# A block of attention and adapters: the row maxima turned by VectorE instead of TensorE and ScalarE, with other places for the side work

## The reference

```python
mod = (silu(c) @ wmod).reshape(4, 6, 1, 256)          # sa, ca, ga, sb, cb, gb
h = layernorm(x) * (1 + ca) + sa
x = x + ga * attention(h)                             # 16 heads of 16 features
h = layernorm(x) * (1 + cb) + sb
x = x + gb * ffn(h)

def attention(h):
    q, k, v = heads(h @ qkv_w.T)
    p = softmax(q @ k.T * 0.25)                       # over 1024 keys
    return merge(p @ v) @ proj_w.T + proj_b

def ffn(x):                                           # x: [batch, 1024, 256] as 16 x 256 x 256 or 4 x 1024 x 256
    h = relu(x @ W_enc + b_enc)                       # 8 experts of 64
    losses = mean((h @ W_dec + b_dec - x) ** 2)       # per batch and expert
    e = argmin(losses)                                # one expert for a batch
    return x @ W_base + b_base + relu(x @ W_down[e] + b_down[e]) @ W_up[e] + b_up[e]
```

## Time and profile before

| | |
|---|---|
| median of three runs | 971.41 us (971.34 to 973.51) |
| the profiled execution | 969.45 us |
| its span | 967.6 us |
| TensorE matmuls, weight loads busy | 933.6 us (96%), 487.8 us (50%) |
| VectorE, ScalarE, GpSimd busy | 791.9 us (82%), 656.6 us (68%), 373.1 us (39%) |
| mean granted clock of TensorE | 0.987 |

### The profile page before, as it was taken

One profiled execution on the slowest core, in us unless ns is written; L12 is line 12 of the kernel. 1 busy time (PEld: TensorE's weight loads), 2 busy tenths in 40 slices (PEclk: granted clock), 3 DMA queues, 4 the chain that ended last, 5 costly groups with the idle time before them and its releaser, 6 DMA issues.

```text
span 967.6 us, 16714 instructions
## 1 busy us (share of the span) xinstructions
PE 933.6 (96%) x5890; PEld 487.8 (50%) x5890; DVE 791.9 (82%) x1629; ACT 656.6 (68%) x1295; POOL 373.1 (39%) x497
## 2 busy tenths in 40 slices
PE   6899999999999999999999999999999999999998
PEld 5443444444445555555454555555445455644486
DVE  4799989999888888877897987876887778888365
ACT  2148788888688677666779677675777766657930
POOL 4050265226456454121756545121655321115320
PEclk9889999999999999999999999999999999999999
DMA  6933052253454211555150511536133500141001
GB/s 179 144 73 45 23 111 63 57 116 87 77 83 74 58 42 36 73 92 162 46 94 13 94 57 36 83 65 167 46 67 51 78 12 25 46 128 55 30 6 50
DMA packets 51427, 68.78 MB, mean 71 GB/s; under 512 B 12347, under 2 KB 35648, under 8 KB 51332
## 3 DMA queue, kind: packets, MB, share of 16 engines
q1 hardware_dynamic: 50108, 66.84, 32.1%
q0 software_dynamic: 384, 0.79, 0.6%
q10 hardware_dynamic: 852, 0.09, 0.1%
HBM read 29.31 MB, written 12.59 MB: 43 GB/s over the span
## 4 chain that ended last, share of the span: by engine, by line
PE 75%; DVE 11%; ACT 5%; DMA 4%; SPq 3%; issue 2%; POOL 1%; ACTq 0%; DVEq 0%
PE pE L851 25%; PE pM L851 21%; PE pO L851 20%; DVE mx L1350 7%; PE pX L851 7%; DMA QO<-lo 2%; ACT P L1176 2%; SPq L1955 1%; DMA xin<-in_x 1%; DVE junk L1544 1%; ACT h2l_full L1263 1%; SPq L2015 1%; DMA P<-in_wmod 0%; ACT h1l_full L1217 0%; DVE junk L1487 0%
## 5 line engine op out<-in xcount | busy, mean ns | idle before, releaser
L1350 DVE TENSOR_REDUCE mx<-pM 128x1 f32<-128x512 f32 x458 | 298.9, 683 | 41.6 <-PE pM L851 39.4
L1176 ACT ACTIVATE P<-pM 128x512 f32<-128x512 f32 x464 | 260.2, 603 | 71.5 <-PE pM L851 70.1
L1350 DVE TENSOR_REDUCE mx<-pE 128x1 f32<-128x512 f32 x428 | 284.5, 682 | 29.4 <-PE pE L851 28.4
L1176 ACT ACTIVATE P<-pE 128x512 f32<-128x512 f32 x413 | 240.6, 603 | 81.0 <-PE pE L851 79.9
L851 PE MATMUL pO<-P,V 128*17 128x512 f32 x2048 | 260.6, 604 | 0.3 <-ACT P L1176 0.2
L851 PE MATMUL pM<-KO,QO 48*128 48x512 f32 x458 | 181.7, 451 | 7.7 <-DMA QO<-lo 6.0
L851 PE MATMUL pE<-KO,QO 48*128 48x512 f32 x428 | 178.4, 444 | 1.4 <-DVE mx L1350 0.6
L851 PE MATMUL pM<-QO,KO 50*128 50x512 f32 x464 | 173.6, 433 | 0.9 <-DVE mx L1350 0.4
L851 PE MATMUL pE<-QO,KO 50*128 50x512 f32 x413 | 169.8, 438 | 1.3 <-DVE mx L1350 0.7
L851 PEld LDWEIGHTS pM<-QO,KO 50*128 50x128 f32 x464 | 80.2, 187 | 85.3 <-issue 59.6
L851 PEld LDWEIGHTS pE<-QO,KO 50*128 50x128 f32 x413 | 73.5, 186 | 96.9 <-issue 76.4
(11 more groups left out here) (362 smaller groups left out, 1392.5 us busy)
## 6 DMA issues: line engine op xcount, KB each, us to landing
outs<-osb SPq DMA_DIRECT2D x31, 256.0 KB, 2.0
KO<-hi SPq DMA_DIRECT2D x56, 128.0 KB, 4.0
QO<-hi SPq DMA_DIRECT2D x56, 128.0 KB, 5.6
x<-in_x SPq DMA_DIRECT2D x20, 256.0 KB, 3.5
out<-x SPq DMA_DIRECT2D x16, 256.0 KB, 2.1
AT<-outs SPq DMA_DIRECT2D x15, 256.0 KB
asum<-wsum SPq DMA_DIRECT2D x15, 256.0 KB
KO<-lo SPq DMA_DIRECT2D x28, 128.0 KB, 4.0
```

Of the source, the lines that this page charges most:

```text
L1176: e.activation(P[:, u % 3, j, :], bank(s), ACT.Exp).then_inc(*empties(s))
L1350: e.tensor_reduce(mx[:, hq % 2, k:k + 1, kh], bank(s), AX.X, ALU.max, negate=True).then_inc(*empties(s))
```

## The change

The step `mturn` is done by VectorE. It reads `mhl` and writes `mT` by four transposes of 32 by 32 elements; there is no matmul, no bank and no copy. A new semaphore `s_mT` counts the turns and takes the place of the bank's semaphores for SyncE, for ScalarE's first two DMAs and for VectorE's own reductions. `mturn` is now a quiet step, put in front of the quiet queue, two units behind `mmax`. Beside that, constants of the order are changed.

```diff
-SHORT = {"ln1turn", "mturn", "oturn", "atturn", "xturn", "select", "modT2"}
+SHORT = {"ln1turn", "oturn", "atturn", "xturn", "select", "modT2"}
-SHARE = (1.3, 1.8, 2.2, 2.4)
+SHARE = (1.3, 1.8, 1.6, 2.4)
-LIGHT = 66
+LIGHT = 68
...
     for gi in range(3, 4 * NB):
-        u = 200 if gi == 4 * NB - 1 else 16 * gi - 33
+        u = 196 if gi == 4 * NB - 1 else 16 * gi - 35
         at(u, ("qk", gi // 4, gi % 4, 0), ("qk", gi // 4, gi % 4, 1))
         if gi > 3:
-            at(u - 9, ("wqload", gi), ("wqs", gi))
+            at(u - 12, ("wqload", gi), ("wqs", gi))
...
-            at(B + 5, ("pick", q), ("select", q), ("fetch", q))
+            at(B + 7, ("pick", q), ("select", q), ("fetch", q))
...
-            u = B + (20 if b == LAST else 53)
+            u = B + (20 if b == LAST else 49)
             at(u, ("prep", b), ("wbload", b))
...
-                at(B + 16, ("ln1load", b + 1, k), ("ln1s", b + 1, k), ("ln1n", b + 1, k), ("ln1turn", b + 1, k), ("h1s", b + 1, k))
-            at(B + 34 if b else B + 18, *(("v", b + 1, k) for k in range(4)))
+                at(B + 10, ("ln1load", b + 1, k), ("ln1s", b + 1, k), ("ln1n", b + 1, k), ("ln1turn", b + 1, k), ("h1s", b + 1, k))
+            at(B + 37 if b else B + 18, *(("v", b + 1, k) for k in range(4)))
...
     if kind == "mturn":
-        return [(("mmax", b), 1.2)]
+        return [(("mmax", b), 2)]
...
     if kind == "qk":
-        return ... + [(("moved", 4 * b + a[0] - 1), 4 if (b, a[0]) == (1, 2) else 3)]
+        return ... + [(("moved", 4 * b + a[0] - 1), 4 if (b, a[0]) == (1, 2) else 2)]
...
     if kind == "ehi":
-        return [(("enc", b, a[0]), 0.5)] + ...
+        return [(("enc", b, a[0]), 0.4)] + ...
...
-                waiting["short"].insert(0, ("mturn", m // 32 - 1))
+                waiting["quiet"].insert(0, ("mturn", m // 32 - 1))
...
-        for _ in range(6 if moving and moving[0][1] == 4 * NB - 1 else 3):
+        for _ in range(6 if moving and moving[0][1] == 4 * NB - 1 else 2):
...
-                elif kind == "mturn":                      # TensorE
-                    pe.wait_ge(s_mhl, s[1] + 1)
-                    e.transpose(o[0:32, 0:128], mhl[:, s[1] % 2, :], ident).then_inc(*fills(s))
...
-                elif kind == "mturn":                      # ScalarE
-                    hq = s[1]
-                    if hq >= 2:
-                        for j in range(4):
-                            act.wait_ge(d_m[hq % 2][j], 16 * (hq // 2))
-                    act.wait_ge(*full(*s))
-                    e.activation(mT[0:32, hq % 2, :], bank(s)[0:32, 0:128], ACT.Copy).then_inc(*empties(s))
-                    if hq == 0:
-                        act.wait_ge(*emptied(*s))
-                        for j in (2, 3):
-                            e.dma_start(*rows(hq, j)).then_inc(d_m[0][j], 16)
+                elif s == ("mturn", 0):
+                    act.wait_ge(s_mT, 1)
+                    for j in (2, 3):
+                        e.dma_start(*rows(0, j)).then_inc(d_m[0][j], 16)
...
                     if hq >= 2:                            # VectorE, before a reduction
-                        dve.wait_ge(*full("mturn", hq - 2))
+                        dve.wait_ge(s_mT, hq - 1)
...
+                elif kind == "mturn":                      # VectorE
+                    hq = s[1]
+                    if hq >= 2:
+                        for j in range(4):
+                            dve.wait_ge(d_m[hq % 2][j], 16 * (hq // 2))
+                    dve.wait_ge(s_mhl, hq + 1)
+                    for k in range(0, 128, 32):
+                        a = e.transpose(mT[0:32, hq % 2, k:k + 32], mhl[k:k + 32, hq % 2, :])
+                    a.then_inc(s_mT, 1)
...
                 elif kind == "mturn":                      # SyncE
-                    sp.wait_ge(*emptied(*s))
+                    sp.wait_ge(s_mT, hq + 1)
                     for j in range(4 if hq else 2):
                         e.dma_start(*rows(hq, j)).then_inc(d_m[hq % 2][j], 16)
```

More of the change, by code:

```diff
@@ L27 @@
           "out": 2}
-BANKED = {"modmm", "modT", "modT2", "ln1turn", "qk", "v", "mturn", "oturn", "atturn", "proj", "xturn", "enc", "gsq",
+BANKED = {"modmm", "modT", "modT2", "ln1turn", "qk", "v", "oturn", "atturn", "proj", "xturn", "enc", "gsq",
           "half", "base", "select", "mid", "out", "setupa", "setupb", "setupq", "setupc"}
-SHORT = {"ln1turn", "mturn", "oturn", "atturn", "xturn", "select", "modT2"}
-QUIET = {"oput", "oget", "orec", "osum", "onorm", "wbload", "gates", "ln1load", "ln1s", "ln1n", "prep", "prepb", "xload", "addx", "bn2", "ln2s", "ln2n", "xsq", "xhi", "xsp", "ehi", "elo", "wsplit", "wload", "sbc", "scale", "pick", "fetch",
+SHORT = {"ln1turn", "oturn", "atturn", "xturn", "select", "modT2"}
+QUIET = {"mturn", "oput", "oget", "orec", "osum", "onorm", "wbload", "gates", "ln1load", "ln1s", "ln1n", "prep", "prepb", "xload", "addx", "bn2", "ln2s", "ln2n", "xsq", "xhi", "xsp", "ehi", "elo", "wsplit", "wload", "sbc", "scale", "pick", "fetch",
          "h1s", "wvload", "wvs", "wqload", "wqs"}
 BURST = 3
-SHARE = (1.3, 1.8, 2.2, 2.4)
-LIGHT = 66
+SHARE = (1.3, 1.8, 1.6, 2.4)
+LIGHT = 68
 LEAD = 50
@@ L159, in before @@
     if kind == "qk":
-        return [(("h1s" if b else "ln1turn", b, 2 * a[1] + i), 0.7) for i in range(2)] + ([(("wqs", 4 * b + a[0]), 0.5)] if b else []) + [(("moved", 4 * b + a[0] - 1), 4 if (b, a[0]) == (1, 2) else 3)]
+        return [(("h1s" if b else "ln1turn", b, 2 * a[1] + i), 0.7) for i in range(2)] + ([(("wqs", 4 * b + a[0]), 0.5)] if b else []) + [(("moved", 4 * b + a[0] - 1), 4 if (b, a[0]) == (1, 2) else 2)]
     if kind == "v":
@@ L199, in before @@
         b_, th_ = former(b, a[0] // 4)
-        return [(("enc", b, a[0]), 0.5)] + ([(x, 0) for x in sums(b_, th_)] if b_ >= 0 else [])
+        return [(("enc", b, a[0]), 0.4)] + ([(x, 0) for x in sums(b_, th_)] if b_ >= 0 else [])
     if kind in ("gsq", "half"):
@@ L698, in adaln_block @@
         s_free = [sem(f"free{i}") for i in range(7)]
-        s_pv = sem("pv")
+        s_pv, s_mT = sem("pv"), sem("mT")
         s_sgexp, s_hi, s_qh, s_ql, s_osb, s_xsq = (sem(n) for n in ("sgexp", "hi", "qh", "ql", "osb", "xsq"))
```

## The result

| | before | after |
|---|---|---|
| median | 971.38 us (22 runs) | 974.96 us (22 runs) |
| ratio | 1 | 1.0028 [1.0015, 1.0041] |
| span of the profiled execution | 967.6 us | 973.1 us |
| mean granted clock | 0.987 | 0.980 |

The changed kernel is 0.28% slower, 3.6 us by the medians, where 964 had been forecast. It lies inside the range, but on the other side of no change: the whole interval is above 1, at about the 0.3% that a measurement can tell.

A forecast was written before the change was run, and what follows sets the result against it. TensorE was taken to set the time, VectorE following closely; -6.7 (TensorE) - 0.4 (ScalarE) + 4.1 (VectorE) - 3.5 (places) = -6.5 us gave 963.0 or 964.9, stated as 964 us, range 951 to 981.

The forecast's parts named there:

- I put a third on the path: Eight turns in the first sequence's light units: a third of VectorE's 0.72 us each delays the kernel, 1.9 us.
- an eighth there: The other 24 turns, where VectorE idles more: an eighth of their work lands on the path, 2.2 us.
- +4.1 us in sum: VectorE's new transposes over all 32 turns: of 23 us of work, 4.1 us land on the path.
- the term of the places: Changed order of steps: half of 7.1 us of TensorE gaps and clock dips is won, -3.5 us.
- The 1.45 us of waits that VectorE had per light period: VectorE's slack between minima in light units: some 1.45 us, more than a 0.72 us turn, but in pieces.
- TensorE and ScalarE, -6.7 - 0.4 = -7.1 us: Removed work: 32 transposes at 0.21 us save TensorE 6.7 us; 32 copies dropped from ScalarE save 0.4 us.
- A turn by VectorE, 0.72 us: Four transposes at 0.18 us without overlap, 0.72 us a turn; low end 0.4 us, high end 1.38 us.
- The stand at 773.25: TensorE's 2.09 us gap for copies of QO stays, as the last group's copies may not start before unit 208.
- the rival through the copies: At two copies a burst, two later groups arrive 3.8 us late, each with a clock dip: 980 us, chance 0.09.
- Slower through VectorE: Transposes at the high end, a wait behind GpSimd, three further gaps with clock dips: +11.3 us, 983 us, chance 0.14.
- faster: More even bursts take a third off the 35.7 us of waits for freed banks, 12 us: 952 us, chance 0.10.
- waits of weight loads for mx clearly over 36 us: Sign that the forecast is wrong: TensorE's weight loads wait longer for VectorE's reductions than 36 us in all.

The follow-up runs named there:

- the order of before: The old kernel's order of steps, with all its constants, queue and distance; with only the turn given to VectorE it took 977.83 us, ratio 1.0058.
- the new places without the lumps: The changed order, mxc as one-operand reduction, the two sbc steps in different bursts; 967.87 us with VectorE's turn, 967.93 with the old, 958.57 with none.
- no_turn: Kernel before with the turn's transposes and copies removed, a constant in the rows they filled; 964.68 us, ratio 0.9917.
- turn_early: Kernel before with only the turns of halves 0 to 9 given to VectorE; 975.03 us, ratio 1.0026.
- after_fixed: Changed kernel with mxc as a one-operand reduction and the two sbc steps never in one burst; 967.87 us, ratio 0.9943; repeated, 968.24 us, 0.9958.
- best_late: Changed places, mxc as one-operand reduction, the two sbc steps in different bursts, VectorE turning only halves 10 to 31; 967.80 us, ratio 0.9951 to before.
- places_mxc_sbc: Changed places with the old turn, mxc as a one-operand reduction and the two sbc steps kept out of one burst; 967.93 us, ratio 0.9955 to before.
- after_mxc: Changed kernel with only mxc made a one-operand reduction; 970.00 us, ratio 0.9983 to before.
- turn_late: Kernel before with only the turns of halves 10 to 31 given to VectorE; 970.16 us, ratio 0.9972.

## Why the prediction was wrong

**The step that failed** is the share of VectorE's work that lands on the path: "I put a third on the path" for eight turns and "an eighth there" for 24, +4.1 us in sum. Measured it was +13.2 us in the order of before, half of the work, and 8.4 us in the new places without the lumps. It failed in two ways. At an equal clock, by the rate above, the turn still costs 9.7 and 6.2 us, so the share itself was too small. And the sum had no term for what a fuller VectorE does to TensorE's clock: dips of 1.8 us stand in the term of the places and in two rivals, none in VectorE's 4.1 us, with no reason given. The remaining 3.5 and 2.8 us are that (9.0 us between the means in the new places). The 1.45 us of waits that VectorE had per light period were there, but I asked whether a turn fits into their sum, and not whether the slack comes where the turn is. By my own rows a burst of 1.89 us has 1.80 us of reductions: a turn of 0.77 us is made good only at 0.09 us a burst, some nine bursts, and each other long piece in that time comes on top. This working was not tested by itself. That the next 26.6 us cost more than the first is measured (29.9 against 13.2 us), but in another order and as part of a longer piece, so it doesn't prove the working either.

**The second thing missed** is the few long pieces that VectorE already had. I took the long `mxc` of the earlier trace rows as a price of a turn in a rival. The turn itself never contended: its 128 transposes took 189 to 204 ns. It was `mxc` that became long, where it fell beside a larger GpSimd product. The products for the scale took no longer than with the old turn and TensorE stood as long behind them (1.5 us), but the clock was lower. With both edits 0.70 to 0.85% goes.

The terms one by one:
- TensorE and ScalarE, -6.7 - 0.4 = -7.1 us: right in size, 7.5 us measured by `no_turn`, 9.5 in the new places. The runs don't part the two.
- A turn by VectorE, 0.72 us: 0.83 us, of which 0.77 delays the next reduction. The Trainium skill (VectorE: DVE Perf Modes, "Two Vector instructions with no wait between them") holds here: four of 199 ns take 0.83 us from start to end, so each is held until the one before has ended, and the low end of 0.4 us was out.
- The places, -3.5 us: 2.7 us measured, all of it with the clock, where I had counted half gaps and half dips. Two details were wrong. The stand at 773.25 "stays", I wrote; it went (the last of the rows of waits above is QO<-lo, waited for once, at the start), so the bound at unit 208 did not decide that stand in the way I read it; which constant removed it was not tested. And copies at two a burst made nothing late: the rival through the copies fell.
- With the measured terms, -7.5 + 13.2 - 2.7 = +3.0 us, against +3.6. This is the sum of the two halves once more, no test of its own.

**The rivals.** "Slower through VectorE" had the right engine and, in part, the right mechanism: waits behind GpSimd, though of `mxc` and not of the turn, and gaps with dips of the clock. It was three times too large (+11.3 us). Its point of decision, 1.45 us, wasn't reached. The third of the waits that "faster" took off went the other way, up by 15.0 us. Of the signs to look for, "waits of weight loads for mx clearly over 36 us" was the right one.

**What stays open.** Why early and late turns by VectorE change the time by +0.26% and -0.28% alone and by +0.58% together, in the order of before; the cheaper `mxc` did not explain it, and the late x is there in `turn_early` too (a wait of 2.0 us). The three intervals, 0.1 to 0.2% to either side, don't cover the 0.6% between. About half of it goes with the clock (mean clock 0.9802 and 0.9846 alone, 0.9783 together).

**A version faster than both**: `after_fixed`, `best_late` and `places_mxc_sbc`, 0.42 to 0.57% faster than before, and not told apart from each other.

## What to carry to other kernels

Work moved to the second fullest engine is priced at the places where it falls; here 4.1 of 23 us (18%) was forecast, half was measured in one order and a third in another, and a second helping cost all of itself. Give the sum a term for TensorE's clock wherever the move can make TensorE stand, and compare the mean clock of all runs, not the dips of two traces. Before giving such a move up, look in the new trace for the few long pieces on that engine: here two one-line edits on two of them turned +0.28% into about -0.5%. Undo the halves of a change separately: they added up (1.0058 x 0.9972 = 1.0030), and showed at once which half was wrong.

## What the runs showed of the hardware

- The minimum of two SBUF operands of 16 columns took 0.175 us, but 2.02 us beside a GpSimd product of 2.18 us; as a reduction of one operand over the same data it took 185 to 189 ns in all 32 places, and 0.18 us beside that same product (`after_mxc`). The Trainium skill (SBUF — State Buffer, "Who interferes with whom") says that a VectorE operation with two SBUF inputs contends with a GpSimd one that reads SBUF, and that one with a single input, outside the two-port modes, does not. Both halves of that are seen here.
- In the changed kernel two stands of TensorE of 1.5 and 1.6 us came with a granted clock of 0.83 in the stretches of 20 us that hold them, 3.4 us lost in each, over twice the stand itself. The same stand of 1.5 us in other executions came with 0.91 or 1.00.
- The clock differs between executions where the work does not: over 60 to 80 us it was 0.83 in the kernel before and 0.74 in `turn_late`, which is the same up to its eleventh half. Over 289 executions, each compared with others of its kernel, 0.001 of mean clock went with 0.67 us.
- Without TensorE's first transposes, in the order of before, a load of x issued at 128.3 to 129.5 us kept the statistics waiting until 134.8 to 135.5 us, where one issued at 129.56 us was in by 133.43, and in `turn_late`, which keeps those transposes, one issued at 130.21 by 133.87. I hadn't expected that removing a transpose changes when a load lands, and the runs don't say why.
